# Zones of three groups on ScalarE, stores of 128 rows for the last three groups, and the group before the last but one turned in two pairs

## The reference

```
w = weights[conditions];  y = einsum('bct,bcd->bdt', x, w)
a = quant_dequant_mxfp4(y);  wq = quant_dequant_mxfp4(weight)
out = x + einsum('mk,nk->mn', a, wq) + bias
```

```
exp = floor(log2(max(amax, tiny))) - 2;  scale = 2 ** exp
q = clip(xb / scale, -6, 6);  lsb = 0.5 if |q| < 2 else 1 if |q| < 4 else 2
return round(q / lsb) * lsb * scale
```

## Time and profile before

| | |
|---|---|
| median of 3 runs | 94.29 us (94.0 to 94.6) |
| the profiled execution | 94.47 us, its span 92.8 us |
| PE, DVE, ACT, POOL busy | 83.4, 83.2, 74.0, 30.4 us |
| granted TensorE clock, mean | 0.996 |
| DMA | 22.68 MB, mean 244 GB/s |

### The profile page before, as it was taken

One profiled execution on the slowest core, in us unless ns is written; L12 is line 12 of the kernel. 1 busy time (PEld: TensorE's weight loads), 2 busy tenths in 40 slices (PEclk: granted clock), 3 DMA queues, 4 the chain that ended last, 5 costly groups with the idle time before them and its releaser, 6 DMA issues.

```text
span 92.8 us, 2145 instructions
## 1 busy us (share of the span) xinstructions
PE 83.4 (90%) x707; PEld 41.0 (44%) x707; DVE 83.2 (90%) x149; ACT 74.0 (80%) x86; POOL 30.4 (33%) x57
## 2 busy tenths in 40 slices
PE   4999695996899999999999999999999999999800
PEld 4996263592482334332533433353443244335400
DVE  1189999999999999999999999999999999999910
ACT  3737279998995959999999999999999967974200
POOL 4367797799779704001200300030030000002200
PEclk9999999999999999999999999999999999999998
DMA  2899499999999999999999699599479929808793
GB/s 29 278 325 284 109 282 294 362 343 297 342 243 331 270 316 308 220 226 239 342 245 324 245 253 206 200 273 234 88 264 231 181 94 275 294 16 219 264 300 128
DMA packets 14555, 22.68 MB, mean 244 GB/s; under 512 B 4178, under 2 KB 4946, under 8 KB 14546
## 3 DMA queue, kind: packets, MB, share of 16 engines
q1 hardware_dynamic: 11744, 17.83, 65.0%
q0 software_dynamic: 2128, 3.68, 18.5%
q10 hardware_dynamic: 674, 1.05, 3.5%
HBM read 11.54 MB, written 8.39 MB: 215 GB/s over the span
## 4 chain that ended last, share of the span: by engine, by line
DVE 48%; PE 20%; issue 3%; DVEq 1%
DVE n_int L698 13%; DVE a L726 8%; DVE top L717 7%; DVE low L686 6%; PE o_ps L388 6%; PE y_ps L388 5%; DVE inv L691 3%; DVE zone L704 2%; PE o_ps L353 2%; DVE amax L668 2%; DVE m L657 2%; DVE m L663 1%; PE y_ps L369 1%; PE o_ps L378 1%; PE o_ps L369 1%
## 5 line engine op out<-in xcount | busy, mean ns | idle before, releaser
L388 PE MATMUL o_ps<-wT,aT 128*128 128x512 bf16 x104 | 24.9, 380 | 0.0
L698 DVE TENSOR_TENSOR n_int<-y_sb,inv 128x1024 int16<-128x1024 f32 (+1 forms) x18 | 19.6, 1100 | 0.3
L341 PE MATMUL y_ps<-x_sb,mix 64*64 64x512 f32 x128 | 17.0, 611 | 2.8 <-DMA x_sb<-in_x_dram 0.9
L520 ACT ACTIVATE z<-y_ps 128x1024 bf16<-128x1024 bf16 x16 | 16.3, 1035 | 3.9 <-PE y_ps L341 3.9
L206 POOL DMA_DIRECT2D mix<-in_L_cond_weights_dram x32 | 17.2, 540 | 5.5 <-issue 4.4
L416 PE MATMUL o_ps<-idle 128*128 128x128 bf16 x206 | 15.7, 243 | 1.2 <-DVE idle L736 1.2
L528 ACT COPY y_sb<-y_ps 128x1024 f32<-128x1024 f32 x16 | 16.3, 1036 | 0.0
L388 PEld LDWEIGHTS o_ps<-wT,aT 128*128 128x128 bf16 x104 | 9.1, 98 | 15.5 <-ACT aT L562 4.1
L416 PEld LDWEIGHTS o_ps<-idle 128*128 128x128 bf16 x206 | 14.1, 110 | 2.9 <-issue 2.6
L317 POOL DMA_DIRECT2D x_sb<-o_sb x5 | 4.5, 891 | 32.9 <-ACT o_sb L553 32.9
L536 ACT ACTIVATE zone<-inv 128x1024 int16<-128x1024 int16 (+1 forms) x13 | 11.9, 937 | 0.3 <-DVE inv L691 0.3
(11 more groups left out here) (60 smaller groups left out, 83.3 us busy)
## 6 DMA issues: line engine op xcount, KB each, us to landing
x_sb<-in_x_dram SPq DMA_DIRECT2D x7, 1024.0 KB, 10.3
out_dram<-x_sb SPq DMA_DIRECT2D x16, 256.0 KB, 4.3
x_sb<-o_sb POOLq DMA_DIRECT2D x5, 512.0 KB, 6.8
out_dram<-x_sb SPq DMA_DIRECT2D x5, 512.0 KB, 2.9
w_sb<-in_L_ffn_weight_dram SPq DMA_DIRECT2D x4, 256.0 KB, 3.8
last_x<-in_x_dram SPq DMA_DIRECT2D x4, 256.0 KB, 8.8
x_sb<-in_x_dram SPq DMA_DIRECT2D x1, 512.0 KB, 6.1
mix<-in_L_cond_weights_dram SPq DMA_DIRECT2D x32, 16.0 KB, 7.1
```

What stands on the lines that cost most here:

```text
L341: last = nc.tensor.matmul(y_ps[HALVES[g], 2 * q + r, :], mix[HALVES[r], (step - 1) * GROUP + n, :], x_tiles(step, n)[HALVES[r], :], start= ...
L388: last = nc.tensor.matmul(o_bank(step, t), aT[:, t, c, :], wT[:, c, :], start=False, stop=(c == KC - 1))
L520: nc.scalar.activation(blocked(columns(z[:, step % 2, :, :], 2 * q, 2)), high_by_place(y_tiles(2 * q, 2)), ACT.Abs, scale=ZONE_GAIN).then_ ...
L698: nc.vector.tensor_tensor(columns(n_int, t, n), columns(y_sb[:, step % 2, :, :], t, n), columns(inv, t, n), ALU.mult).then_inc(n_done, 1)
```

## The change

- `ALL_ZONES`: in steps 1, 2 and 7 ACT computes the zone of both pairs, and DVE's `other_zones` is left out. In step 2 DVE's `limit` moves ahead of `block_max`, in step 7 its `tree_1` of group 8 in between the two roundings.
- Group 6: DVE limits and multiplies in two pairs; PE turns each pair when its `a2` is there.
- `SWAPPED`: for groups 6, 8 (both pairs) and 7 (first pair) x and the table rows are loaded with the halves exchanged, so that the mix puts them right. x of these is loaded in pairs, two DMAs of 64 rows for an exchanged pair; the results of groups 6, 7 and 8 are stored in 128 rows, one DMA where there were two. The second pair of group 7 is stored by SP and not by POOL. `last_x` comes in one DMA.
- Group 8: tiles 0 and 1 are zoned, rounded, limited and multiplied as one pair; ACT copies group 7's first pair (`copy_late`) behind the first of the zones; DVE's `add_late` move ahead; PE takes the FFN of tiles 0 and 1, and behind them turns tiles 2 and 3. SP stores tiles 0, 2 and the second half of 3, ACT tile 1 and the first half of 3.

The diff, cut to what is spoken of:

```diff
+    ALL_ZONES = (1, 2, LAST - 1)
+
+    SWAPPED = {LAST - 2: (0, 1), LAST - 1: (0,), LAST: (0, 1)}
...
+                tile, half = first + i // 2, i % 2
+                if tiles.start // 2 in SWAPPED.get(step, ()):
+                    tile, half = first + i % 2, i // 2
...
-        def store_last(queue, t, g, part, done):
-
-            queue.dma_start(exchanged_dram[LAST - 1, t // 2, g, t % 2, :, part], last_x[HALVES[g], t, part]
-                            ).then_inc(done, 16)
+        def store_last(queue, t, part, done):
+            queue.dma_start(out_dram[:, (LAST - 1) * GROUP + t, part], last_x[:, t, part]).then_inc(done, 16)
...
+            def load_x_pair(step, q):
+                n0 = (step - 1) * GROUP + 2 * q
+                place = x_tiles(step, 2 * q, 2).rearrange("p (n t) -> p n t", n=2)
+                if q in SWAPPED[step]:
+                    for r in range(2):
+                        sp.dma_start(place[HALVES[r], :, :], swapped_x_dram[step - 1, q, r, :, :, :]
+                                     ).then_inc(x_in[step], 16)
+                else:
+                    sp.dma_start(place, x_dram[:, n0:n0 + 2, :]).then_inc(x_in[step], 16)
...
+            for t in range(SUMMED, GROUP):
+                sp.wait_ge(added, t - SUMMED + 1)
+                store(LAST - 1, t)
+            for t in range(0, GROUP, 2):
                 sp.wait_ge(added, t + 3)
-                store_last(sp, t, 0, slice(0, N), stored)
-            for half in range(2):
-                sp.wait_ge(added, GROUP + 2 + half)
-                store_last(sp, GROUP - 1, 0, n_half(half), stored)
+                store_last(sp, t, slice(0, N), stored)
+            sp.wait_ge(added, GROUP + 3)
+            store_last(sp, GROUP - 1, n_half(1), stored)
...
+                else:
+                    for q in range(2):
+                        pe.wait_ge(a2_done, late_part(q))
+                        turn_pair(step, q, straight=True)
...
-            ffn_tile(LAST, 0)
-            turn_last(2)
-            ffn_tile(LAST, 1)
-            turn_last(3)
+            for t in range(2):
+                ffn_tile(LAST, t)
+            for t in range(2, GROUP):
+                turn_last(t)
...
+            def step_zones(step):
+                limits = after(step - 1) if step < LAST - 1 else late_part(1)
+                zone_pair(after(step), limits)
+                if step in ALL_ZONES:
+                    zone_pair(after(step), limits, 2, 2, done=other_zone_done)
...
-            for t in range(GROUP):
-                zone_pair(after(LAST), late_part(1), t, 1)
+            zone_pair(after(LAST), late_part(3), 0, 2)
             copy_late()
+            for t in range(2, GROUP):
+                zone_pair(after(LAST), late_part(3), t, 1)
...
+                else:
+
+                    tree_3(step + 4)
+                    limit(step, after(step), 0, 2)
+                    other_zones(step)
+                    rescale(step, late_part(0), 2 * step + 3, 0, 2)
+                    block_max(step + 3)
+                    limit(step, after(step), 2, 2)
+                    lowest_zone(step + 3)
+                    rescale(step, late_part(1), 2 * step + 3, 2, 2)
...
+            round_y(LAST, 0, 2)
+            limit(LAST, after(LAST), 0, 2)
+            round_y(LAST, 2, 1)
+            rescale(LAST, late_part(4), 2 * LAST + 2, 0, 2)
+            limit(LAST, after(LAST) + 1, 2, 1)
+            add_late(2)
+            round_y(LAST, 3, 1)
+            rescale(LAST, late_part(5), 2 * LAST + 3, 2, 1)
+            limit(LAST, after(LAST) + 2, 3, 1)
+            add_late(3)
+            rescale(LAST, late_part(6), 2 * LAST + 4, 3, 1)
```

More of the change, by code:

```diff
@@ L143, in high_by_place, with x_loads @@
             return rows.bitcast(BF16).rearrange("p (b h l two) -> p h b l two", h=HI, l=LO, two=2)[:, :, :, :, 1]
+        def x_loads(step):
+            return 1 if step not in SWAPPED else 2 + len(SWAPPED[step])
         def y_tiles(t, n):
@@ L162, in late_part @@
         def late_part(part):
-            return after(LAST - 1) + part
+            return after(LAST - 2) + part
         def n_half(half):
@@ L205, in load_mixes @@
             for i, row in enumerate(rows):
-                queue.dma_start(mix[HALVES[i % 2], first + i // 2, :],
+                tile, half = first + i // 2, i % 2
+                if tiles.start // 2 in SWAPPED.get(step, ()):
+                    tile, half = first + i % 2, i // 2
+                queue.dma_start(mix[HALVES[half], tile, :],
                                 table[bass.ds(row, 1), :, :].rearrange("o c d -> (o c) d")).then_inc(done, 16)
-        def store_last(queue, t, g, part, done):
-            queue.dma_start(exchanged_dram[LAST - 1, t // 2, g, t % 2, :, part], last_x[HALVES[g], t, part]
-                            ).then_inc(done, 16)
+        def store_last(queue, t, part, done):
+            queue.dma_start(out_dram[:, (LAST - 1) * GROUP + t, part], last_x[:, t, part]).then_inc(done, 16)
         @block.sync
@@ L245, in _ @@
                 load_mixes(sp, mybir.EngineType.SP, sp_mix_in[step], step, SP_TILES)
-                if step + 1 <= STEPS:
+                if step + 1 < LAST - 2:
                     load_x(step + 1)
[L248 to L252, removed]
+                elif step + 1 <= LAST:
+                    for q in range(2):
+                        load_x_pair(step + 1, q)
+            sp.dma_start(last_x[:, :, :], x_dram[:, (LAST - 1) * GROUP:LAST * GROUP, :]).then_inc(last_x_in, 16)
             for step in range(1, LAST):
@@ L258, in _ @@
                     sp.wait_ge(late_copied, 2)
-                store_exchanged(step, 0)
+                if step in SWAPPED:
+                    store(step, 0, SUMMED)
+                else:
+                    store_exchanged(step, 0)
                 if step < LAST - 2:
@@ L331, in mix_pair @@
                 elif q == 0:
-                    pe.wait_ge(x_in[step], 16)
+                    pe.wait_ge(x_in[step], 16 * x_loads(step))
                     pe.wait_ge(pool_mix_in[step], 16 * MIXES // 2)
@@ L449, in _ @@
                     bias_pair(step, 0, start=True)
-                pe.wait_ge(a2_done, after(step))
-                for q in range(2):
-                    turn_pair(step, q, straight=(q == 0 or step == LAST - 2))
+                if step < LAST - 2:
+                    pe.wait_ge(a2_done, after(step))
+                    for q in range(2):
+                        turn_pair(step, q, straight=(q == 0))
+                else:
+                    for q in range(2):
+                        pe.wait_ge(a2_done, late_part(q))
+                        turn_pair(step, q, straight=True)
                 if step == 1:
@@ L593, in _ @@
                 copy_w(t)
-            zone_pair(after(1), after(0))
+            step_zones(1)
             for q in range(2):
@@ L599, in _ @@
                 if step > 1:
-                    zone_pair(after(step), after(step - 1))
+                    step_zones(step)
                 z_pair(step + 2, 0)
@@ L614, in _ @@
                 copy_turned(step, 1)
-            zone_pair(after(LAST - 1), after(LAST - 2))
+            step_zones(LAST - 1)
             y_pair(LAST, 1)
@@ L621, in _ @@
             copy_turned(LAST - 1, 1)
-            for t in range(GROUP):
-                zone_pair(after(LAST), late_part(1), t, 1)
+            zone_pair(after(LAST), late_part(3), 0, 2)
             copy_late()
+            for t in range(2, GROUP):
+                zone_pair(after(LAST), late_part(3), t, 1)
             for t in range(GROUP):
                 copy_turned_last(t)
[L627 to L632, removed]
+            act.wait_ge(added, 4)
+            store_last(act, 1, slice(0, N), others_stored)
+            act.wait_ge(added, GROUP + 2)
+            store_last(act, GROUP - 1, n_half(0), others_stored)
         @block.vector
@@ L792, in _ @@
                     lowest_zone(step + 3)
-                else:
+                elif step in ALL_ZONES:
+                    tree_3(step + 4)
+                    limit(step, after(step))
+                    block_max(step + 3)
+                    rescale(step, after(step), 2 * step + 3)
+                    lowest_zone(step + 3)
+                elif step < LAST - 2:
                     tree_3(step + 4)
@@ L805, in _ @@
             round_y(LAST - 1, 0)
+            tree_1(LAST)
             round_y(LAST - 1, 2)
-            tree_1(LAST)
-            other_zones(LAST - 1)
             tree_2(LAST + 3)
@@ L819, in _ @@
             invert(LAST + 2)
[L822 to L831, removed]
+            round_y(LAST, 0, 2)
[9 more added lines that the diff above has]
+            rescale(LAST, late_part(6), 2 * LAST + 4, 3, 1)
+            dve.wait_ge(last_x_in, 16)
             for t in range(GROUP - 1):
```

34 lines of the change are left out of this document (16 added, 18 removed).

## The result

The changed kernel takes 93.41 us (median of 8 runs, 93.01 to 95.32) against 94.42 for the kernel before (94.0 to 94.88). The ratio is 0.9889, with a 95% interval of 0.9862 to 0.9916: 1.1% faster, clear of noise. The 95.32 is one execution in a slower state (granted clock 0.982), which the ratio leaves out; the highest of the other seven is 93.85. I had forecast no change (94.3). The range, 93.4 to 95.3, just holds the median; the forecast of no change did not come true.

What follows compares the result with a forecast made beforehand. The prediction took PE's stream, from the turn of step 1 on, to set the pace. Its terms, 0.44 (zones) + 0.40 (last group) - 0.9 (stores), summed to -0.1, giving 94.3 us, with a range of 93.4 to 95.3.

Steps and rivals of the forecast that it cites:

- Stores, -0.9: Tail of the last group: the rearranged stores shorten the end by 0.9 us.
- The queueing of issues: Tail: the last store, issued 1.0 us after its data were there, would now leave right behind the last addition.
- I take the same as before: Tail: from the last store's issue to the span's end stays 3.4 us, though the store is now 128 rows.
- What bounds the kernel: From the turn of step 1 on, PE's stream sets the pace; DVE's work costs it only 0.17 us.
- The first rival: DVE sets the pace, so its 1.02 us of zones comes off: 93.3 to 93.7 by the median; chance 0.22.
- Zones, +0.61 at step 1, +0.44 at step 6: Zones added to ACT make PE's turn 0.61 us late at step 1, and 0.44 late at step 6.
- DVE reaches step 8 some 0.2 sooner, and PE gains nothing by it: Step 7's moved zone (0.34) pays the 0.14 of group 6's halves; DVE's earlier arrival is worth nothing to PE.
- DVE's wait at step 3: At the head of step 3 DVE waits 0.7 us for z of step 4, which ACT writes late.
- Group 6 in two pairs, worth 0 and at most the 0.17: Step 6: turning the first pair sooner gains 0, at most 0.17 us, as PE is the late engine.
- Last group, +0.40: Last group: with both turns behind both FFNs, PE has nothing to cover ACT's copy of tile 2: 0.40 us later.
- Clock: Rival: PE's clock falls in the longer gap before step 3's mix, about 2 us more, 96; chance 0.05.
- The slower rival on the tail: The tail gives nothing back: a longer last landing or late `a2` of tile 3, 94.8 to 95.3; chance 0.19.

Runs made afterwards that it cites:

- e1: Kernel before, with only the last group's stores made 128 rows wide and the loads of its x and table rows that this needs: 93.52 us, ratio 0.992.
- e10: Kernel before with all of the change's loads and stores, compute in the old order: 92.73 us, ratio 0.985.
- e12: Kernel before without the 34 filler matmuls around PE's turn of step 1: 94.44 us, ratio 1.000.
- e5: Changed kernel with the second zones of steps 1 and 2 back on DVE, only step 7's on ACT: 93.27 us, ratio 0.988.
- e8: Changed kernel with PE waiting for both pairs of group 6 before turning any: 93.34 us, ratio 0.989.
- e4: Changed kernel with PE's old order in the last group, FFNs and turns alternating: 92.79 us, ratio 0.983.
- e2: Changed kernel with the last group's stores cut into 64 rows, lower half on SP, upper half on ACT: 94.42 us, ratio 1.001.
- e3: Changed kernel with each last-group store cut into two of 64 rows, both on the queue that had the whole: 94.50 us, ratio 1.002.
- e11: e4 without the 14 and 20 filler matmuls around PE's turn of step 1: 92.50 us, ratio 0.980.

## Why the prediction was wrong

The profiled execution was forecast at -0.1 and came out at -1.2. Of the difference, 0.9 is the stores and 0.4 the zones; the last group goes the other way by 0.1.

*Stores, -0.9.* This term was mis-sized most: -1.80. The queueing of issues, which was in the sum, came as forecast: the last issue went from 1.0 behind the last addition to 0.1. The step that failed is "I take the same as before", for the 3.4 us from the last issue to the end: it measured 2.5 (89.0 to 91.5). I had bounded it by landings of 2.7 to 3.4, and by 2.9 for 512 KB in 128 rows; the stores landed in 2.1. The Trainium skill (Trainium Kernel Development and Optimization, Best Practices) says to tile to all 128 partitions. The prediction put this aside, on the ground that the slow narrow stores lie under computation; the tail agrees with it, with ratios of 0.992 (e1) and 0.985 (e10).

*What bounds the kernel.* The step that says that PE's stream alone sets the pace and DVE costs it only 0.17 us failed. The periods were right (8.32 in all runs with the fillers). But at group 7's first pair PE's row touches the one before it, and I took that for a full stream, where the start was given by DVE: 0.84 behind the multiplication, as in e12, e10 and e5. I had both rows and did not set the one against the other. With 2 us less of PE (e12) the time stayed at 94.44, where this step asks for 93.2 to 93.5.

The first rival, that DVE has the pace, had the better mechanism for the kernel before (e12). Its price, 1.02 us, did not come: the added zones make PE late by nearly what they save it later, and DVE itself gains nothing between its multiplications of groups 1 and 7 (50.88 and 50.93 us): of the 0.68 taken out there, 0.40 went into the wait at step 3, 0.14 into the halves, and the rest is not traced. That its 93.3 to 93.7 holds the measured 93.41 is luck. It put the stores at 0.1 to 0.2, and they gave 1.8.

*Zones, +0.61 at step 1, +0.44 at step 6.* The chain ACT, mix, filler, turn was right: the mix of step 3 is 0.91 later behind ACT's zone. The turn of step 1 is 0.41 later and not 0.61, since the last filler lets PE go 0.16 ahead of its recorded end, so DVE's wait was 0.5 and not 0.34. Then 0.15 came back at step 6 (8.02 to 7.87) and 0.21 at group 7's first pair (7.12 to 6.91), against 0.17 in the sum. The net is 0.05, where +0.44 was forecast. The step "DVE reaches step 8 some 0.2 sooner, and PE gains nothing by it" is where the second was lost.

*DVE's wait at step 3.* It was right in place, and 0.32 to 0.40 in size where I had 0.7.

*Group 6 in two pairs, worth 0 and at most the 0.17.* This was right on both sides: 0 by e8, where the zones have made PE late, and the 0.15 of step 6 in e5.

*Last group, +0.40.* The mechanism was right; the size is 0.52 (e4: 0.50).

*Clock.* The granted clock stayed at 1.00 with a gap of 1.51 us; that rival is out. The slower rival on the tail is out as well: landings fell.

## What to carry to other kernels

Where two engines are level, put the start of the waiting instruction against the start of the one that feeds it, and compare that distance with places of known waiting; an empty bracket does not say that nobody waited. Work moved off one of them is worth little while the move delays the other, so time the data movement and the compute parts of such a change apart: here the loads and stores alone came out at 92.73 and the whole at 93.41. At the end of a kernel nothing covers the stores, so try there, and in the groups just ahead, one store of all 128 rows for two of 64, and judge a full DMA by its bytes and not by its share.

## What was not expected of the hardware

- A store of 64 rows took 0.47 to 0.89 us to issue from SP or ACT in the last group, one of 128 rows and the same or twice the bytes 0.33 to 0.38, but for single ones of 0.43 to 0.87.
- With DMA shares of 0.97 to 1.04, stretches of 1 us from 87 on moved 193 to 352 GB/s with the last group stored in 64 rows, and 336 to 391 with it stored in 128.
- The landing of the last group's stores, 64 to 256 KB, went from 3.1 to 2.1 us (medians). Both the width and what was stored ahead go with it (e1, e10, e2, e3); the mechanism is open, and e11's landings of 2.9 with 128-row stores stay unexplained.
